# Building the edge lists by src of a two-layer graph network: 392 scatters of single edges, or 28 scatters of runs of 48

## The reference, cut to what matters

```python
def layer0(x, src, dst, W, att_src, att_dst, bias):          # N = 3125 nodes, E = 50000 edges, 4 heads of 256
    xp = (x @ W).reshape(N, H, C)
    a_src = jnp.einsum('nhc,hc->nh', xp, att_src)
    a_dst = jnp.einsum('nhc,hc->nh', xp, att_dst)
    e = jax.nn.leaky_relu(a_src[src] + a_dst[dst], 0.2)      # src, dst with a loop of each node appended
    ...                                                      # softmax of e over the edges of one dst
    out = jax.ops.segment_sum(xp[src] * alpha, dst, N)
    return jax.nn.relu(out + bias)

def layer1(x, W, a, src, dst):
    h = x @ W
    e = jnp.exp(-jax.nn.leaky_relu((h @ a_l)[src] + (h @ a_r)[dst], 0.1))
    rowsum = jax.ops.segment_sum(e, src, N)
    h_prime = jax.ops.segment_sum(e[:, None] * h[dst], src, N)
    return jax.nn.elu(h_prime / (rowsum[:, None] + 1e-5))

x = x + layer0(jnp.maximum(layernorm(x), 0), ...)
x = x + layer1(jnp.maximum(layernorm(x), 0), ...)
```

## Time and profile before

| | us |
|---|---|
| median of three runs | 2250.3 |
| the profiled execution | 2243.8 |
| its span | 2242.3 |
| stage `lists_and_project`, to the next stage's first DMA issue | 678.9 |
| POOL busy in the span | 1366.9 |
| PE busy in the span | 1697.4 |
| DVE busy in the span | 1131.4 |

### The profile page before, as it was taken

One profiled execution on the slowest core, in us unless ns is written; L12 is line 12 of the kernel. 1 busy time (PEld: TensorE's weight loads), 2 busy tenths in 40 slices (PEclk: granted clock), 3 DMA queues, 4 the chain that ended last, 5 costly groups with the idle time before them and its releaser, 6 DMA issues. The chain is left out here.

```text
span 2242.3 us, 27665 instructions
## 1 busy us (share of the span) xinstructions
PE 1697.4 (76%) x10226; PEld 925.2 (41%) x10226; DVE 1131.4 (50%) x2763; ACT 401.0 (18%) x791; POOL 1366.9 (61%) x1296
## 2 busy tenths in 40 slices
PE   3685937668812878888777987845899999999997
PEld 2332413224301544545444544521355544445454
DVE  5564824548611566677676676652333333333331
ACT  1111201111100121222211222211222222122221
POOL 1566675567776566666676666207676666676740
PEclk9787967879965777777778777766998999999898
DMA  7221402203208999999999999629999999999971
GB/s 226 67 58 41 116 23 61 69 27 111 70 19 333 329 347 341 348 359 366 355 363 346 352 352 369 199 78 405 380 352 352 361 351 355 353 373 349 365 247 43
DMA packets 186965, 561.17 MB, mean 250 GB/s; under 512 B 45714, under 2 KB 50167, under 8 KB 186469
## 3 DMA queue, kind: packets, MB, share of 16 engines
q0 software_dynamic: 139776, 416.40, 51.8%
q1 hardware_dynamic: 43448, 129.78, 17.0%
q10 hardware_dynamic: 3600, 13.16, 1.6%
HBM read 554.33 MB, written 53.28 MB: 271 GB/s over the span
## 5 line engine op out<-in xcount | busy, mean ns | idle before, releaser
L940 POOL DMA_INDIRECT ring<-layer_rows,idx x360 | 412.5, 1146 | 230.8 <-PE acc L1065 114.4
L412 POOL DMA_INDIRECT src_lists<-pay_T,slot_T x392 | 407.8, 1040 | 214.9 <-issue 129.9
L1503 POOL DMA_INDIRECT ring<-layer_rows,idx x360 | 366.6, 1018 | 184.7 <-issue 91.8
L508 PE MATMUL mm<-w_sb,hT 128*128 128x512 f32 x800 | 381.5, 627 | 26.9 <-issue 26.8
L1065 PE MATMUL acc<-ring,weight 128*32 128x256 f32 (+1 forms) x3600 | 329.0, 485 | 6.7 <-DVE weight L1172 3.7
L508 PEld LDWEIGHTS mm<-w_sb,hT 128*128 128x128 f32 x800 | 157.6, 202 | 215.5 <-issue 215.5
L1565 PE MATMUL acc<-ring,weight 128*32 128x512 f32 x1600 | 213.2, 628 | 36.6 <-ACT weight L1513 19.1
L1065 PEld LDWEIGHTS acc<-ring,weight 128*32 128x32 f32 (+1 forms) x3600 | 149.7, 137 | 125.9 <-issue 83.6
L1665 DVE TENSOR_TENSOR hT_low<-tp_l,hT_high 128x512 fp32r<-128x512 f32 x50 | 34.6, 691 | 316.5 <-issue 223.5
L1016 PE MATMUL turned<-ident,edge_a 128*16 128x128 f32 (+1 forms) x125 | 38.8, 311 | 193.9 <-ACT edge_a L952 93.7
L1598 PE MATMUL mm_l<-w_high,hT_high 128*128 128x512 f32 x400 | 169.3, 423 | 4.6 <-issue 2.6
(11 more groups left out here) (232 smaller groups left out, 2184.4 us busy)
## 6 DMA issues: line engine op xcount, KB each, us to landing
layer_rows<-row_l ACTq DMA_DIRECT2D x25, 514.0 KB
layer_rows<-row_l SPq DMA_DIRECT2D x25, 514.0 KB
own<-layer_rows SPq DMA_DIRECT2D x25, 512.0 KB
x<-xb SPq DMA_DIRECT2D x25, 512.0 KB
x1t<-x SPq DMA_DIRECT2D x25, 512.0 KB
xt<-in_x_dram SPq DMA_DIRECT2D x24, 512.0 KB
xb<-in_x_dram SPq DMA_DIRECT2D x24, 512.0 KB
out_dram<-y SPq DMA_DIRECT2D x24, 512.0 KB
```

The source lines that it names most:

```text
L412: pool.indirect_dma_start(out=list_d, out_offset=bass.IndirectOffsetOnAxis(ap=slot_T[:, b:b + 1], axis=0), in_=pay_T[:, b:b + 1], in_offse ...
L508: last = pe.matmul(mm[k][:, f * HALF:(f + 1) * HALF], hT[k][:, c, :], w_sb[:, c, f * HALF:(f + 1) * HALF], start=c == 0, stop=c == KC - 1)
L940: pool.indirect_dma_start(out=ring[:, t % 2, blocks(c), :][:, q, :], out_offset=None, in_=table0, in_offset=bass.IndirectOffsetOnAxis(ap=i ...
L1503: pool.indirect_dma_start(out=fetched(t, c)[:, q, :], out_offset=None, in_=table1, in_offset=bass.IndirectOffsetOnAxis(ap=idx, axis=0), bo ...
```

## The change

Instead of giving every edge its place in DRAM, the kernel packs a chunk's edges first. For each chunk c and group w, the edges of c that belong to w are laid side by side in a row of 48 elements on partition w. One scatter of 100 such rows then writes all lists at the places to which they are filled so far.

- `rank_chunk` starts the scan anew for each chunk, so ranks count within the chunk. Two small operations keep where each list stands (`bases`) and where the row of 48 is to be written (`starts`); they take the place of the copy of `carry`.
- `spread_chunk` (new, DVE) takes the place of `slot_chunk`. It makes two one-hot arrays of a chunk's 1792 edges in f16: to which group an edge belongs (`of_window`, 128 x 14 x 100) and at which of 48 spots it is to stand (`at_spot`, 128 x 14 x 48), and two products of the latter with the edge's value, which is split into two fields of 10 bits (`parts`).
- `pack_runs` (new, PE): 14 matmuls per chunk of `of_window` with `parts` (96 columns), summed in PSUM.
- `keep_run` (new, DVE): the two fields are put together again (`run`, 100 x 48).
- `scatter` on POOL: one indirect DMA per chunk; each waits until the one before has landed, because a row of 48 also overwrites the places behind its own edges, which the next chunk fills.
- Values are stored as their difference from the "no edge" value, so an empty place is 0. A list's region in DRAM is 864 long in place of 640, and it is filled with zeros by two DMAs in place of one. `lists_by_src` takes the greater of the two neighbours' shared pieces, and subtracts back.
- The chunks of a step use one PSUM bank (`aux[0]` for ranks, `aux[1]` for packed rows), and steps are one later for the last part: ranks turned in step i + 1, spread and packed in i + 2, kept and scattered in i + 3.

```diff
+SPAN = 48
+REGION = CAP + 2 * SPAN + P
+FIELD = 1024
...
             def scatter(c):
-                pool.wait_ge(slots_done, c + 1)
-                for b in range(c * CB, (c + 1) * CB):
-                    pool.indirect_dma_start(
-                        out=list_d, out_offset=bass.IndirectOffsetOnAxis(ap=slot_T[:, b:b + 1], axis=0),
-                        in_=pay_T[:, b:b + 1], in_offset=None,
-                        bounds_check=last_slot, oob_is_err=False).then_inc(scattered, 16)
+                pool.wait_ge(runs_done, c + 1)
+                if c >= 1:
+                    pool.wait_ge(scattered, 16 * c)
+                pool.indirect_dma_start(
+                    out=list_d, out_offset=bass.IndirectOffsetOnAxis(ap=starts[:, c:c + 1], axis=0),
+                    in_=run[c % 2][:, :], in_offset=None).then_inc(scattered, 16)
...
+            def pack_runs(c):
...
+                pe.wait_ge(spread_done, c + 1)
+                if first >= 1:
+                    pe.wait_ge(runs_done, first)
+                for i in range(CB):
+                    last = pe.matmul(packed_at(c), of_window[c % 2][:, i, :],
+                                     parts[c % 2][:, i, :, :].rearrange("p k n -> p (k n)"),
+                                     start=i == 0, stop=i == CB - 1)
+                last.then_inc(packed_done, 1)
...
                 for c in chunks_of(i - 1):
                     add_ranks(c)
+                for c in chunks_of(i - 2):
+                    pack_runs(c)
...
-                then(dve.tensor_copy(carry[:, :], running[:, CW - 1:CW]), scanned)
+                then(dve.scalar_tensor_tensor(out=bases[:, c + 1:c + 2], in0=running[:, CW - 1:CW],
+                                              scalar=bases[:, c:c + 1], in1=full[:, :], op0=ALU.add, op1=ALU.min), scanned)
+                then(dve.scalar_tensor_tensor(out=starts[:, c:c + 1], in0=bases[:, c:c + 1], scalar=sign[0:NWP, :],
+                                              in1=region0[0:NWP, :], op0=ALU.mult, op1=ALU.add), scanned)
...
+            def spread_chunk(c):
...
+                if c >= 2:
+                    dve.wait_ge(packed_done, c - 1)
+                then(dve.tensor_tensor(of_window[k][:, :, :], along(win_T[:, cols], NWP), across(windows[:, :], NWP),
+                                       ALU.is_equal), place_math)
+                dve.wait_ge(ranked, end)
+                then(dve.tensor_tensor(place_f[:, :], aux[0][:, (c - first) * CB:(c - first + 1) * CB], way[:, cols], ALU.mult), place_math)
+                then(dve.tensor_tensor(place[:, :], place_f[:, :], way0[:, cols], ALU.add), place_math)
+                then(dve.tensor_tensor(at_spot[:, :, :], along(place[:, :], SPAN), across(spots[:, :], SPAN),
+                                       ALU.is_equal), place_math)
+                then(dve.tensor_tensor(parts[k][:, :, 0, :], at_spot[:, :, :], along(high_T[:, cols], SPAN), ALU.mult),
+                     place_math)
+                then(dve.tensor_tensor(parts[k][:, :, 1, :], at_spot[:, :, :], along(low_T[:, cols], SPAN), ALU.mult),
+                     spread_done)
...
+            def keep_run(c):
...
+                dve.wait_ge(packed_done, end)
+                if c >= 2:
+                    dve.wait_ge(scattered, 16 * (c - 1))
+                then(dve.tensor_copy(run[k][:, :], packed_at(c)[:, SPAN:2 * SPAN]), place_math)
+                dve.scalar_tensor_tensor(out=run[k][:, :], in0=packed_at(c)[:, 0:SPAN], scalar=float(FIELD),
+                                         in1=run[k][:, :], op0=ALU.mult, op1=ALU.add).then_inc(runs_done, 1)
...
+                for c in chunks_of(i - 3):
+                    keep_run(c)
                 for c in chunks_of(i - 2):
-                    slot_chunk(c)
+                    spread_chunk(c)
```

More of the change, by code:

```diff
@@ L208, in lists_and_project @@
         placed = [sb(f"placed{k}", [NWP, CW], F16) for k in range(2)]
-        carry = sb("carry", [NWP, 1])
+        bases = sb("bases", [NWP, CHUNKS + 1])
+        starts = sb("starts", [NWP, CHUNKS], U32)
+        full = sb("full", [NWP, 1])
+        sign = sb("sign", [P, 1])
+        region0 = sb("region0", [P, 1])
+        run = [sb(f"run{k}", [NWP, SPAN]) for k in range(2)]
         first = sb("first", [NWP, 1])
@@ L233, in lists_and_project @@
         junk_last = sb("junk_last", [P, PAIRS], BF16)
-        over = sb("over", [P, CB])
-        turned_rank = sb("turned_rank", [P, CB])
         sw_T = sb("sw_T", [P, BLK], I32)
-        odd_T = sb("odd_T", [P, BLK], I32)
-        way = sb("way", [P, BLK])
-        slot0 = sb("slot0", [P, BLK])
-        slot_T = sb("slot_T", [P, BLK], U32)
-        pay_T = sb("pay_T", [P, BLK])
+        pay_T = sb("pay_T", [P, BLK], I32)
+        field_T = sb("field_T", [P, BLK], I32)
+        win_T = sb("win_T", [P, BLK], F16)
+        high_T = sb("high_T", [P, BLK], F16)
+        low_T = sb("low_T", [P, BLK], F16)
+        way = sb("way", [P, BLK])
+        way0 = sb("way0", [P, BLK])
+        place_f = sb("place_f", [P, CB])
+        place = sb("place", [P, CB], F16)
+        windows = sb("windows", [P, NWP], F16)
+        windows_i = sb("windows_i", [P, NWP], I32)
+        spots = sb("spots", [P, SPAN], F16)
+        of_window = [sb(f"of_window{k}", [P, CB, NWP], F16) for k in range(2)]
+        at_spot = sb("at_spot", [P, CB, SPAN], F16)
+        parts = [sb(f"parts{k}", [P, CB, 2, SPAN], F16) for k in range(2)]
         w_t = [sb(f"w1_t{k}", [P, D]) for k in range(2)]
@@ L316, in chunks_of, with group, packed_at @@
             return [c for c in range(CHUNKS) if c * (TILES - 1) // CHUNKS - 1 == i]
+        def group(c):
+            own = next(g for g in (chunks_of(i) for i in range(-1, TILES)) if c in g)
+            return own[0], own[-1] + 1
+        def packed_at(c):
+            n = c - group(c)[0]
+            return aux[1][0:NWP, 2 * n * SPAN:2 * (n + 1) * SPAN]
         @block.sync
@@ L681, in rank_chunk, with along, across @@
                     .then_inc(placed_done, 1)
-            def slot_chunk(c):
+            def spread_chunk(c):
+                k = c % 2
+                first, end = group(c)
                 cols = slice(c * CB, (c + 1) * CB)
-                dve.wait_ge(ranked, c + 1)
-                then(dve.tensor_tensor(turned_rank[:, :], aux[c % 2][:, 0:CB], way[:, cols], ALU.mult), slot_math)
-                then(dve.tensor_scalar(over[:, :], aux[c % 2][:, 0:CB], CAP + 0.5, 1.0e6, ALU.is_gt, ALU.mult), slot_math)
-                then(dve.tensor_tensor(over[:, :], over[:, :], turned_rank[:, :], ALU.add), slot_math)
-                then(dve.tensor_tensor(slot_T[:, cols], over[:, :], slot0[:, cols], ALU.add), slots_done)
+                def along(line, n):
+                    return line.rearrange("p (b o) -> p b o", o=1).to_broadcast([P, CB, n])
+                def across(line, n):
+                    return line.rearrange("p (a n) -> p a n", a=1).to_broadcast([P, CB, n])
+                if c >= 2:
[11 more added lines that the diff above has]
+                     spread_done)
@@ new lines, in keep_run @@
+            def keep_run(c):
+                k = c % 2
+                _, end = group(c)
+                dve.wait_ge(packed_done, end)
[4 more added lines that the diff above has]
+                                         in1=run[k][:, :], op0=ALU.mult, op1=ALU.add).then_inc(runs_done, 1)
@@ L714, in _ @@
                                           in1=order[:, 1:1 + RUNS], op0=ALU.mult, op1=ALU.add), consts)
+            then(dve.tensor_scalar(sign[:, :], shift[:, :], -2.0, 1.0, ALU.mult, ALU.add), consts)
+            then(dve.tensor_scalar(region0[:, :], shift[:, :], float(OWN * P - SPAN), None, ALU.mult), consts)
+            then(dve.scalar_tensor_tensor(out=region0[:, :], in0=wid[:, :], scalar=float(REGION), in1=region0[:, :],
+                                          op0=ALU.mult, op1=ALU.add), consts)
+            then(dve.memset(full[:, :], float(CAP)), consts)
+            then(dve.memset(bases[:, 0:1], 0.0), consts)
+            then(dve.tensor_copy(windows[:, :], windows_i[:, :]), consts)
+            then(dve.tensor_copy(spots[:, :], iota[:, 0:SPAN]), consts)
             then(dve.tensor_scalar(shift[:, :], shift[:, :], float(WIN), None, ALU.mult), consts)
@@ L740, in _ @@
                 score(i)
+            for c in chunks_of(TILES - 3):
+                keep_run(c)
             merge_shared()
@@ L1288, in lists_by_src @@
 def lists_by_src(nc, list_d, ident, found, found_last, shift, idx1, idx1_first, loc1, flag):
+    PW = NWP // 2
+    SHARED = P + 2 * SPAN
     with ExitStack() as ctx:
```

90 lines of the change are left out of this document (57 added, 33 removed).

## The result

The changed kernel took 2118.7 us (median of four runs, 2113.56 to 2124.55), the kernel before beside it 2247.61 (four runs, 2233.66 to 2277.98). The ratio is 0.9447, 95% interval 0.9388 to 0.9506: faster. 2118 was predicted. The profiled execution took 2124.55 us.

A forecast was written before the change was run, and what follows sets the result against it. Bound: PE's stalls plus a POOL tail in the first stage. DVE's loop end 527 plus 8 of waits, next stage 543.5 against 678.9 (-135), about 1 and 4 us back: -130, so 2118 us; range 2072 to 2190.

The forecast's parts named there:

- At that end POOL alone is late: End of the first stage: POOL still scatters after PE and DVE are done, late by about 37 us.
- Both come from the 392 scatters: First stage: PE's stalls (five stretches adding up to 180 us) and the POOL tail both come from the scatters.
- rival B: First stage: part of PE's stalls stays, as something else than the scatters starts them; about 2182 us, chance 0.12.
- 28 scatters were priced at 1.1 us: POOL, first stage: 28 scatters of 100 runs at about 1.1 us, 31 us in place of 408.
- 4.43 us for the four wide operations: DVE, per chunk: one comparison and three products at the slower price, 1.70 + 3 x 0.91 us.
- Rival A: DVE: the f16 products run at the dense price, 53 us less, PE bounds; about 2078 us, chance 0.10.
- 0.8 us per chunk: PE, first stage: the 14 added matmuls of 96 columns take 0.8 us per chunk, making a tile 15.8 us.
- The 8 us of waits: DVE's loop: 8 us added for the last two tiles (2) and the falling clock (the rest), loop end 535.
- 7.8 us from the last scatter to the next stage: End of the first stage: the same 7.8 us as in the kernel before, next stage at 543.5 us.
- C: First stage: the stalls are PE's own and stay whole; about 2247 us, no change, chance 0.10.
- D: First stage: PE's own stalls stay and also slow the 14 added matmuls per chunk; 2361 us, chance 0.06.
- E: A chunk with more than 48 edges of one group sends the kernel down the dense path; no chance of its own.

The follow-up runs named there:

- b_no_scatter: The kernel before without its 392 scatters, so only the first stage is to be read: 1944.01 us, next stage at 453.9 us.
- before_again: The kernel before, unchanged, measured again on chip 5: 2091.98 us, next stage at 616.1 us.
- a_keep_first: The changed kernel with `keep_run` ahead of the iteration's statistics in place of behind them, on chip 10: 2032.45 us.
- a_window_twice: The changed kernel with `of_window` computed twice per chunk, on chip 5: 2077.56 us, next stage 43.8 us later.
- experiment 11: The test of a_keep_first (2032.45 us) against the changed kernel; its 3.02 us scatter is from the unchanged kernel before on chip 5.

## Why the prediction was right, and where it was not

*The bound.* Two readings. "At that end POOL alone is late": shown, by b_no_scatter (the tail goes with the scatters) and by before_again (it is there without any stall). The 37 us that I read were only what the stalls had left of it: without them POOL ends some 162 us late. "Both come from the 392 scatters": half of it was not shown. In the later measurements, on chips 5 and 10, as dense a stream made no stall. What supports it is one comparison within the first measurement: "issue" idle went from 119 us to 0 in the one stage that lost its indirect DMAs, and stayed in the two that kept theirs. That is one profiled execution of each kernel. I also wrote, against rival B, that the gathers' stages stall little; measured against chip 5 both kernels lose some 90 us there (1563.4 against 1474.2 before, 1571.7 against 1479.6 after). I had looked only at PE's small matmuls and had no undisturbed trace to compare with.

*So the size was right for that measurement alone.* On chip 5 60 us were gained of the 130 forecast, and the same working would have been 3% off ((130 - 60) / 2092). The start of the next stage after the change was forecast about equally well for both (543.5 against 551.3 and 551.5); what doesn't carry over is the 678.9 that it was subtracted from. No experiment met such stalls again, so what starts them is open: the chip, something that went on beside the kernel at that time, or these together with indirect DMAs. That the sum held in the first measurement rests on both kernels having been measured under the condition of the profile.

*POOL.* 28 scatters were priced at 1.1 us and took 1.98, since most start beside `of_window`; undisturbed they take 0.99 (the last one), near the price. Hidden either way: a_keep_first gave the 25 us of POOL back and the time stood still.

*DVE in and out.* 4.43 us for the four wide operations: 1.61 + 3 x 0.86 and gaps, 4.3. The two small operations of `keep_run` 0.17 and 0.21, the two of `rank_chunk` 0.22 each: the guess of 0.20 held. Iteration 16.88 (scatters at 127.32 and 144.20) against 17.0. Rival A is out: no operation ran at the dense price in this layout.

*PE.* 0.8 us per chunk; the row has 0.81 to 0.83 in two places of the timeline:

```profile
522.74 0.83 PE L566 MATMUL aux<-parts,of_window 128*100 128x96 f16 x14
...
537.21 0.81 PE L566 MATMUL aux<-parts,of_window 128*100 128x96 f16 x14
```

but 27.8 / 28 = 0.99 in the mean: the one at 504.46, after PE had waited 11.95 us, took 1.43. DVE did become the bound, as a_window_twice shows.

*The 8 us of waits.* This term was mis-sized. The loop ended at 543, not at 535. DVE waited 14.5 us for x tiles and 2.5 for ACT's last rows; 9.4 of these lie at one place:

```profile
484.04 0.33 SPq L418 DMA_DIRECT2D w_t<-in_L_gnn_W_dram  x1
484.41 0.29 SPq L359 DMA_DIRECT2D xt<-in_x_dram  x1
...
497.47 1.29 DVE L620 BATCH_NORM_STATS2 stats<-xt 128x6 f32<-128x512 f32 x2 [9.38 <-DMA xt<-in_x_dram]
```

On SP the load of the last tile stands behind a load of `w_t`, which waits until DVE has scored what its buffer held. ACT was done with the buffer that the tile goes into at 456.2:

```profile
454.91 1.24 ACT L472 ACTIVATE ht<-xt,nbias_l,rstd_l 128x1024 f32<-128x1024 f32 x1 [5.39 <-DVE nbias_l L631]
```

So the queue held the load back by 28 us, until 484.4. The load itself was slow too: DVE started on it 13.1 us after its issue, where the tile before took 4.6 (issued at 463.86, started on at 468.42); why is not shown. I had counted the clock and the last tiles, and neither of these. In the kernel before DVE waited for x tiles only 4.1 us in its loop in the first measurement, but 14.7 on chip 5, where nothing stalled.

*The rest.* 7.8 us from the last scatter to the next stage: 8.0. "About 1" for the two loads of `lists_by_src` and 4 left for short stalls: the later stages took 8.3 more in the first measurement and 5.4 on chip 5 (1.8 and 3.6). So the two profiled executions are 119.3 us apart (2243.8 to 2124.55), and not 130: 7.3 of the error in the stage (127.7 for 135), 3.3 behind it. The medians are 128.9 apart, because the profiled execution of before lay 4 us below its median and that of the changed kernel 6 above. That 2118 was hit to the microsecond is that chance.

*Rivals.* B came true for the stages behind, in both kernels alike, and not for this one. C and D are out: the changed stage ends at 551 us in both measurements, and no pair of the new matmuls met a stall. E didn't arise.

## What to carry to other kernels

A stall whose rows name no releaser is first to be looked for in another execution, on another chip if there is one: what isn't there doesn't come from the program alone, however well it goes along with one of its engines. When work is moved from POOL to an engine that has slack, look for the next limit: here it was DVE. And a layout that suits one engine's fast price is to be priced at its reader too: nearly halving the price of DVE's four wide operations put 50 us on PE, and 10 us came back, not 45.

## What was not expected of the hardware

- The same kernel took 2247 us in one measurement and 2090 in others, with runs of 2233.66 to 2277.98 and of 2087.72 to 2097.76. The difference shows as idle time, much of it named "issue"; in the changed kernel the DVE operation above took 691 ns in both, POOL's gathers in `attend` 1120 and 1114.
- Matmuls with a step of 28 bytes in one operand, either one, had rows of 0.35 us in place of 0.24.
- An indirect DMA's own time on POOL doubled (0.99 to 2.08 us) when it started beside `of_window`, a DVE operation with two inputs in SBUF. The next such operation held it up further where it followed the first without a gap (3.02 us, experiment 11), and not where it began 0.45 us after the first had ended (145.88, `at_spot`, before the scatter's end at 146.29).
